# Two accumulating transfers per tile in place of GpSimd's additions, one state buffer per slot, and the last residuals kept on chip

## What is computed

```python
u = silu(conv(h) + b)                               # 512 inner channels
delta_lr, Bm = split(u @ x_proj_w.T + x_proj_b)     # Bm: 16 states
delta = softplus(delta_lr @ dt_w.T + dt_b)
deltaA = exp(einsum('bld,dn->bldn', delta, A))
deltaBu = einsum('bld,bln->bldn', delta * u, Bm)
def step(carry, inp):
    dA, dBu = inp
    carry = dA * carry + dBu
    return (carry, carry.sum(-1))                   # sum over the 16 states
y = ys + u * D_param
x = x + (y @ out_w.T + out_b)
```

## Time and profile before

| | us |
|---|---|
| median of 3 runs | 1076.79 |
| lowest and highest of them | 1074.73 and 1078.74 |
| the profiled execution, its own time | 1079.94 |
| its span, first to last instruction | 1078.2 |
| PE busy in the span | 959.9 (89%) |
| DVE busy | 897.8 (83%) |
| POOL busy | 859.3 (80%) |
| ACT busy | 755.8 (70%) |
| mean granted TensorE clock | 0.968 of full speed |

### The profile page before, as it was taken

The page is one execution under the profiler, slowest core; times in us unless marked ns, Lnnn a source line. Parts: engine busy times, 40 slices in busy tenths (PEclk is TensorE's granted clock), DMA queues, the critical chain, the costliest instruction groups (busy, mean ns, idle before and its releaser), DMA issues.

```text
span 1078.2 us, 13117 instructions
## 1 busy us (share of the span) xinstructions
PE 959.9 (89%) x4210; PEld 511.9 (47%) x4210; DVE 897.8 (83%) x1210; ACT 755.8 (70%) x1321; POOL 859.3 (80%) x617
## 2 busy tenths in 40 slices
PE   8786997999899999999889999899899999686976
PEld 6452453444545454545445454546355454432554
DVE  2433697899998999899989999799989999899944
ACT  2346558778698769877797769876887869765634
POOL 1357898988889888898889898889889888999700
PEclk9996999999999999999999999999999999899999
DMA  9813440434142430545042521344053202200000
GB/s 339 315 55 157 157 177 20 176 118 169 48 153 103 177 118 21 195 138 196 20 175 99 179 78 68 149 157 177 21 196 109 88 1 118 99 0 1 15 25 20
DMA packets 22059, 124.72 MB, mean 116 GB/s; under 512 B 3495, under 2 KB 4135, under 8 KB 9448
## 3 DMA queue, kind: packets, MB, share of 16 engines
q1 hardware_dynamic: 16376, 89.09, 22.7%
q10 hardware_dynamic: 5616, 34.81, 8.4%
HBM read 115.23 MB, written 8.65 MB: 115 GB/s over the span
## 4 chain that ended last, share of the span: by engine, by line
DVE 24%; POOL 21%; ACT 20%; PE 18%; issue 12%; DMA 4%; SPq 1%; ACTq 1%; DVEq 0%; POOLq 0%
POOL state L601 13%; DVE state L880 12%; PE bank L1013 10%; PE acc L1013 6%; ACT decay L668 5%; POOL state L609 4%; DVE raw L863 3%; DVE hm L943 2%; ACT u L759 2%; ACT soft L654 2%; DVE sg L930 2%; ACT L668 2%; ACT hid L654 2%; POOL x_in L570 2%; ACT u L767 1%
## 5 line engine op out<-in xcount | busy, mean ns | idle before, releaser
L601 POOL TENSOR_TENSOR state<-w,brep 128x512 f32<-128x512 f32 (+1 forms) x352 | 614.2, 1770 | 34.4 <-PE acc L1013 34.0
L880 DVE TENSOR_TENSOR_SCAN state<-decay,state 128x512 f32<-128x512 f32 (+1 forms) x352 | 590.7, 1696 | 44.6 <-ACT decay L668 26.1
L1013 PE MATMUL acc<-state,ident 128*128 128x512 f32 x832 | 406.8, 610 | 13.2 <-DVE state L880 9.3
L668 ACT ACTIVATE decay<-delta,neg_a 128x496 f32<-128x496 f32 x512 | 328.6, 671 | 97.8 <-DVE state L880 97.2
L1013 PEld LDWEIGHTS acc<-state,ident 128*128 128x128 f32 x832 | 150.4, 194 | 161.9 <-issue 118.8
L609 POOL TENSOR_TENSOR state<-state 128x512 f32<-128x512 f32 x96 | 122.3, 1274 | 29.5 <-DVE state L880 28.9
L695 ACT ACTIVATE sg<-bank,ag 128x512 f32<-128x512 f32 x64 | 43.5, 680 | 63.3 <-PE bank L1013 63.3
L1013 PE MATMUL bank<-xn_t,in_w 128*128 128x512 f32 x128 | 61.9, 619 | 13.1 <-ACT xn_t L716 7.8
L632 POOL TENSOR_TENSOR w<-delta,u 128x512 f32<-128x512 f32 x32 | 40.3, 1271 | 34.1 <-ACT delta L791 34.1
L1013 PE MATMUL bank<-out_w,u 128*128 128x256 f32 x256 | 58.0, 382 | 6.7 <-DVE u L871 6.7
L930 DVE SCALAR_TENSOR_TENSOR sg<-sg,bank 128x512 f32<-128x512 f32 x64 | 43.1, 674 | 18.2 <-ACT sg L695 18.2
(11 more groups left out here) (142 smaller groups left out, 1336.8 us busy)
## 6 DMA issues: line engine op xcount, KB each, us to landing
keys<-in_keys_t SPq DMA_DIRECT2D x32, 1028.0 KB, 4.8
keys<-in_keys_n SPq DMA_DIRECT2D x32, 1024.0 KB
brep<-b_scratch ACTq DMA_DIRECT2D x32, 1024.0 KB, 6.2
x_scratch<-x_in SPq DMA_DIRECT2D x8, 512.0 KB, 2.6
res<-x_scratch SPq DMA_DIRECT2D x8, 512.0 KB, 4.6
out<-res SPq DMA_DIRECT2D x8, 512.0 KB, 4.3
x_in<-in_x SPq DMA_DIRECT2D x7, 512.0 KB, 5.3
brep<-in_w_gateT SPq DMA_DIRECT2D x1, 1024.0 KB, 14.1
```

The costliest lines, as they stand in the source:

```text
L601: nc.gpsimd.tensor_tensor(state[state_buffer(odd, g)][:, 0:count, :], w[:, m, :].unsqueeze(1).to_broadcast((P, count, TOK)), brep[:, n:n + ...
L668: last = nc.scalar.activation(decay[:, to + i, :, 1:LEN], d, ACT.Exp, scale=neg_a[:, m, n + i:n + i + 1])
L880: nc.vector.tensor_tensor_scan(flat, decay[:, of:of + count, :, :].rearrange("p c q l -> p (c q l)"), flat, 0.0, ALU.mult, ALU.add).then_i ...
L1013: return nc.tensor.matmul(o, l, r, start=first, stop=last)
```

## The change

- `PAIRED` and POOL's additions are gone. `MERGED = {2: 0, 6: 4}`: when slot 2 is scanned, POOL issues a DMA transfer that reads both states of slot 0's buffer and adds them to the two states in slot 2's buffer; the same from slot 4 to slot 6. There are two of 512 KB per tile, 64 in the whole run, each waiting for the one before it. They are issued three slots behind POOL's inputs (`MERGE_LAG`).
- PE sums slots 2 and 6 four slots after their place (`MERGED_LAG`), with two matmuls each, and slots 0 and 4 not at all. That is 16 - 4 = 12 matmuls per tile. Those of slot 6 now stand together with slot 10's at the tile's end.
- State buffers: one per slot number, 11 of them, of one or two states.
- The residuals of the last two blocks are neither stored nor loaded; they stay in `x_in`, which `x2`, `stats3`, `xn3`, `finish` and the output store use in phases 8 and 9.
- `POST`, `PRE`, `LAST` and `PREPARE` have other steps for most parts.

```diff
 POST = [
-    ("x2", [4, 5]),  ("y_last", [0]),  ("finish", [32, 66, 76, 83]),
+    ("x2", [5, 5]),  ("y_last", [1]),  ("finish", [31, 65, 79, 84]),
 PRE = [
-    ("add1", [40]),  ("add2", [63]),  ("x_proj", [67]),  ("x_dbl", [72]),
-    ("dt", [73, 78, 85, 87]),  ("b_load", [77, 79, 79, 87]),
+    ("add1", [28]),  ("add2", [71]),  ("x_proj", [71]),  ("x_dbl", [73]),
+    ("dt", [75, 78, 87, 87]),  ("b_load", [77, 80, 87, 87]),
 PREPARE = [
-    ("quantise", [29, 48, 54, 57]),
+    ("quantise", [22, 57, 61, 72]),
...
-PAIRED = (2, 4, 6)
-PAIR_LAG = 4
-SUMS = [[k for k in range(CPT) if k + 2 * (k in PAIRED) == c] for c in range(CPT)]
+MERGED = {2: 0, 6: 4}
+MERGE_LAG, MERGED_LAG = 3, 4
+SUMS = [[k for k in range(CPT) if k not in MERGED.values() and k + MERGED_LAG * (k in MERGED) == c]
+        for c in range(CPT)]
...
-        state = [sb(f"state{i}", [P, 2, TOK]) for i in range(RING)]
+        state = [sb(f"state{c}", [P, SCAN[c][2], TOK]) for c in range(CPT)]
...
-                if post:
+                if post and pre:
                     reach(sp, out_stored, j - 2, 0)
                     sp.dma_start(res[:, :, :], t["x1_scratch"][j - 2]).then_inc(res_loaded, 16)
...
-                    reach(sp, res_biased[1], j, 1)
-                    sp.dma_start(t["x1_scratch"][j], x_in[par][:, :, :]).then_inc(x1_stored, 16)
+                    if j < BLOCKS - 2:
+                        reach(sp, res_biased[1], j, 1)
+                        sp.dma_start(t["x1_scratch"][j], x_in[par][:, :, :]).then_inc(x1_stored, 16)
...
-                        user = g - RING
-                        reach(pool, summed, *((b, sums_to(user)) if user >= 0 else (b - 1, sums_to(user + SLOTS))))
+                        user = g - CPT
+                        of, user = (b, user) if user >= 0 else (b - 1, user + SLOTS)
+                        if merge_from(user) is not None:
+                            reach(pool, merged, of, 16 * merges_to(merge_from(user)))
+                        else:
+                            reach(pool, summed, of, sums_to(user))
...
-                        done = g - PAIR_LAG
-                        if done >= 0 and done % CPT in PAIRED:
+                        done = g - MERGE_LAG
+                        if done >= 0 and done % CPT in MERGED:
+                            more = done - done % CPT + MERGED[done % CPT]
                             reach(pool, scan_done, b, done + 1)
-                            s = state[state_buffer(odd, done)]
-                            nc.gpsimd.tensor_tensor(s[:, 0, :], s[:, 0, :], s[:, 1, :], ALU.add).then_inc(paired, 1)
+                            if merges_to(done) > 1 or b:
+                                reach(pool, merged, b, 16 * (merges_to(done) - 1))
+                            nc.gpsimd.dma_start(state[done % CPT][:, :, :], state[more % CPT][:, :, :],
+                                                accum_op=ALU.add).then_inc(merged, 16)
...
-                            if k in PAIRED:
-                                reach(pe, paired, b, pairs_to(s))
+                            if k in MERGED:
+                                reach(pe, merged, b, 16 * merges_to(s))
                             else:
                                 reach(pe, scan_done, b, s + 1)
-                            for i in range(1 if k in PAIRED else SCAN[s][2]):
+                            for i in range(SCAN[s][2]):
```

More of the change, by code:

```diff
@@ L54 @@
-    ("out_proj", [2, 2]),
-    ("hidden", [15, 18, 21, 30, 43, 50, 64, 69]),
-    ("finish", [32, 66, 76, 83]),
-    ("x_evac", [13]),
-    ("scale_x", [12]),
-    ("down", [32, 57, 74, 80]),
+    ("x2", [5, 5]),
+    ("gate", [15, 17, 19, 23, 42, 50, 57, 69]),
+    ("xn3", [10]),
+    ("x_turn", [6]),
+    ("y_last", [1]),
+    ("rstd3", [4]),
+    ("stats3", [6]),
+    ("x_evac", [13]),
+    ("scale_h", [22, 33, 69, 79]),
+    ("out_proj", [2, 4]),
+    ("h_floor", [20, 31, 62, 76]),
+    ("h_scale", [22, 32, 69, 78]),
@@ L60 @@
+    ("h_evac", [30, 35, 75, 81]),
+    ("scale_x", [11]),
+    ("down", [32, 61, 78, 84]),
+    ("x_max", [10]),
+    ("h_turn", [26, 34, 72, 81]),
+    ("finish", [31, 65, 79, 84]),
+    ("tanh", [14, 18, 20, 22, 38, 49, 58, 68]),
+    ("h_max", [19, 29, 53, 71]),
+    ("up", [9, 14, 17, 22, 36, 46, 50, 67]),
+    ("hidden", [15, 18, 19, 26, 43, 51, 63, 69]),
 ]
 PRE = [
-    ("xn1", [5]),
-    ("query", [6]),
-    ("exp", [13, 19, 29, 37]),
-    ("softplus", [84, 87]),
-    ("x_dbl", [72]),
-    ("turn2", [55]),
@@ L86 @@
[L86 to L101 removed]
+    ("attn_out", [45, 47]),
@@ new lines @@
+    ("turn2", [54]),
+    ("evac2", [56]),
+    ("u_evac", [60, 61, 63, 65]),
+    ("xn2", [54]),
+    ("turn1", [4]),
+    ("p_evac", [18, 27, 31, 41]),
+    ("exp", [13, 22, 27, 38]),
+    ("softplus", [83, 87]),
+    ("p_sum", [19, 25, 31, 44]),
+    ("rstd1", [0]),
+    ("p_turn", [15, 25, 31, 40]),
+    ("zt_evac", [25, 29, 38, 44]),
+    ("add1", [28]),
+    ("p_last", [15, 24, 29, 38]),
+    ("tap0", [59, 61, 64, 65]),
+    ("add2", [71]),
+    ("attend", [23, 26, 32, 41]),
+    ("stats1", [2]),
@@ new lines @@
+    ("z_turn", [24, 27, 35, 44]),
+    ("mix_in", [57, 58, 59, 62]),
+    ("s_max", [13, 15, 25, 32]),
+    ("z_evac", [24, 27, 33, 43]),
+    ("xn1", [3]),
+    ("rstd2", [53]),
+    ("x_dbl", [73]),
+    ("times_u", [81, 87, 87, 87]),
+    ("s_neg", [13, 17, 25, 35]),
+    ("query", [5]),
+    ("stats2", [52]),
+    ("tap2", [59, 62, 65, 65]),
+    ("x1", [50, 51]),
+    ("evac1", [6]),
+    ("s_bias", [13, 19, 26, 38]),
+    ("x_proj", [71]),
+    ("dt", [75, 78, 87, 87]),
+    ("silu", [62, 65, 65, 65]),
@@ L121 @@
[L121 to L128 removed]
+    ("scale_x", [3]),
+    ("h_evac", [28, 41, 71, 80]),
+    ("h_floor", [26, 37, 57, 73]),
+    ("out_proj", [1, 11]),
+    ("hidden", [14, 24, 27, 36, 41, 53, 56, 72]),
+    ("h_scale", [29, 38, 72, 74]),
+    ("h_max", [25, 36, 56, 72]),
@@ L129 @@
+    ("x_evac", [5]),
+    ("x_turn", [11]),
+    ("down", [36, 39, 73, 74]),
+    ("x_max", [12]),
+    ("finish", [40, 44, 74, 74]),
+    ("x2", [1, 3]),
+    ("h_turn", [32, 38, 69, 69]),
+    ("stats3", [11]),
+    ("xn3", [1]),
+    ("y_last", [0]),
+    ("gate", [13, 14, 24, 28, 40, 44, 49, 70]),
+    ("tanh", [6, 14, 26, 26, 32, 41, 56, 56]),
+    ("rstd3", [11]),
+    ("scale_h", [26, 30, 58, 58]),
+    ("up", [21, 21, 26, 29, 36, 49, 50, 56]),
 ]
@@ L140 @@
 PREPARE = [
-    ("quantise", [29, 48, 54, 57]),
+    ("abs_sum", [5, 14, 14, 27]),
+    ("vo", [11]),
+    ("quantise", [22, 57, 61, 72]),
     ("vo_rep", [8]),
-    ("qk", [6]),
-    ("total", [35]),
-    ("scales", [42]),
-    ("vo", [7]),
-    ("vo_evac", [38]),
-    ("mixer_weights", [29]),
-    ("abs_sum", [8, 22, 24, 39]),
+    ("mixer_weights", [25]),
+    ("total", [27]),
+    ("scales", [36]),
+    ("vo_evac", [25]),
+    ("qk", [4]),
 ]
@@ L181, in sums_to, with merges_to, merge_from @@
     m, c = divmod(g, CPT)
-    return m * len(SUM_SLOTS) + SUM_SLOTS.index(c + 2 * (c in PAIRED)) + 1
-def pairs_to(g):
+    return m * len(SUM_SLOTS) + SUM_SLOTS.index(c + MERGED_LAG * (c in MERGED)) + 1
+def merges_to(g):
     m, c = divmod(g, CPT)
-    return m * len(PAIRED) + PAIRED.index(c) + 1
+    return m * len(MERGED) + list(MERGED).index(c) + 1
+def merge_from(g):
+    m, c = divmod(g, CPT)
+    return next((m * CPT + to for to, of in MERGED.items() if of == c), None)
 def slots_to(n):
```

105 lines of the change are left out of this document (20 added, 85 removed).

## The result

The changed kernel takes 1122.9 us (1122.2 to 1131.8) beside 1076.1 (1074.7 to 1078.7) for the one before: a ratio of 1.044, with a 95% interval of 1.041 to 1.047. It is 47 us slower; 12.5 us faster were forecast. The profiled execution took 1122.15, its span is 1120.3.

A forecast was written before the change was run, and what follows sets the result against it. No engine alone was taken as the bound: PE slightly latest, DVE right behind. Phases 2 to 7 gave 8.4 us less, phase 1 4, phase 8 1.5, tail 1.4 more: 12.5 less, median 1064; 8-in-10 range 1040 to 1096.

The forecast's parts named there:

- Other parts: Moved POST and PRE steps, quantise parts, residuals and tail; reordering priced 0, with 1 us a block either way.
- The period of a block: Steady block of 119.10 us: DVE becomes longest, block 2.4 us less before lateness; ends 0 and 5.2.
- The block: Steady block in phases 2 to 7: 2.4 less, minus 0.8 and 0.2 for transfers; marks about 117.7 us apart.
- POOL: Per block twelve additions (15.3 us) go, eight issues of 1.27 come: net 5.1 us less, 99.7 busy.
- Rival 2: An issue costs POOL more than the additions did, above 1.9 us; at 3.0 the total is 1093; chance 0.08.
- That wait costs nothing: POOL's wait for a scan at each merge is free while an issue stays under 5.7 us.
- The landing: An adding transfer lands in 4.6 to 6.2 us, 5.9 to 7.5 with its issue, hidden in most tiles.
- Rival 1: Transfers land too late, over 10.6 us after the scan, in six of ten of 32 tiles: 1096; chance 0.18.
- 0.8 + 0.2 a block: Late y at a block's last tile costs 0.8 us; shared DMA engines between output store and x2 0.2.
- Phase 1: First phase, where POOL leads: POOL's 5.1 us less are worth 4.
- The residuals: Dropped stores and loads of the last two residuals: worth 0.3 us, at the last x2.
- The tail: End of the last scan: y written 1.7 us later through slot 6's landing, net 1.4 more; ends -1 and 4.

The follow-up runs named there:

- a2: The kernel before with the changed kernel's four tables (POST, PRE, LAST, PREPARE), nothing else; 1126 us, ratio 1.048.
- d1: The kernel before with the whole new PRE table; 1141 us, ratio 1.059.
- b3: The kernel before with two PRE entries as in the changed one, attn_out [45, 47] and turn2 [54]; 1097.9 us, ratio 1.019.
- d4: b1 with slot 0's first state summed as well, 13 matmuls per tile in place of 12; 1098.5 us, ratio 1.020.
- b1: a4 with slots 2 and 6 summed in their own place, not four slots later; 1121.6 us, ratio 1.040.
- e1: The changed kernel with PE summing slot 0's first state, the transfer to slot 2 adding only the second; 13 matmuls per tile; 1132.5 us, ratio 1.053.
- d3: The kernel before without POOL's additions and its waits for them, three second states missing from the sum; 1074 us, ratio 0.998.
- b4: a3 with POOL's wait for the scans at the merges put back, still no transfers; 1109.6 us.
- a3: The changed kernel without its 64 transfers and POOL's scan waits for them, four of sixteen states missing from the sum; 1107.9 us, ratio 1.030.
- c3: The kernel before with only the residuals of its last two blocks kept in x_in; ratio 0.9999.
- d2: The kernel before with the new LAST and PREPARE tables alone; ratio 1.004.
- a4: a3 with the four tables of the kernel before; 1141 us, ratio 1.062.
- a1: The changed kernel with the four tables of the kernel before, transfers kept; 1173 us, ratio 1.091.
- c2: The kernel before with one spare matmul ahead of the first scores; 1076.2 us, ratio 1.0008.
- b2: The changed kernel with four spare matmuls in PE's gap ahead of turn2, in phases with a scan; 1112.2 us, ratio 1.030.
- c1: b2 with one more spare matmul, ahead of the first scores; 1113.3 us.
- e2: e1 with slot 4's first state summed directly too, both transfers 256 KB, 14 matmuls per tile; 1132.9 us, ratio 1.053.

## Why the prediction was wrong

**The step that failed** is the one under "Other parts": "The moved steps of POST and PRE are the same operations in another order; I take 0". By a2 the tables alone cost 52 us, by d1 `PRE` alone 64, and by b3 two of its entries 21. The trace before already had the place: the timeline of PE at `turn2` had 1.35 us of idle time behind ten records of sums, and the prediction didn't read it. Where "1 us a block either way" was allowed, a2 shows 6.9 (126.0 against 119.1).

**The step behind it** is "The period of a block": PE's 3.9 us less was taken as room for the others, with 0 as its worst end ("when other waits fill what PE frees"). That fewer sums could cost time was in no term and no rival. The sums are PE's filling between the stages of other work: one taken out of a place where PE waits for a chain of other engines frees nothing, and the clock can fall. The prediction read the clock as 0.99 and priced no fall of it. PE was to be busy 107.6 a block and was 111.0; its work did fall by the 3.9, and 3.5 of that came back as work at the lower clock. d4 against b1 is this step alone, in the old tables: one sum less per tile is 23 us slower. It isn't so in every order: e1 has one sum more than the changed kernel and is 10 us slower.

Point by point:
- The block: 117.7 forecast (1.4 less than 119.1), 124.2 measured. DVE, which was to become the longest, is busy 110 a block as before and idles 14.1 a block in place of 9.1.
- PE's records on `acc`: 768, as forecast. Price of 0.969 per matmul right at the upper level of the clock.
- POOL: the additions' 122.3 us went, 64 issues of 0.96 came where 1.27 was taken. A block is 7.9 us less in phases 2 to 7 ((629.6 - 582.0)/6) where 5.1 was said. Right in kind, and worth 2.7 us in all (d3). Rival 2, a dear issue, is out: no issue took over 1.18.
- "That wait costs nothing": right. POOL now waits 155.7 us for scans at the merges, and b4 shows that to be free.
- The landing, 4.6 to 6.2 forecast: 4.7 at the median, and 4.5 to 10.6 over the run. Rival 1 asked for over 10.6 us after the scan in six of ten tiles; it is one of the eight transfers of a block that lands so late. The forecast put the late one at the block's last tile behind the B loads. At the end of phase 1 it was right: landing in 9.54, 2.98 of waiting by PE, 4.49 by DVE. In phases 2 to 7 the late one was in the middle of the block, behind the keys and `x_in`; the last tile's landed in 6.0 to 6.7, and its y, now behind a scan, doesn't wait. The sum had 0.8 + 0.2 a block for them; the runs show 15 us in all (after against a3), of which 1.6 a block in phases 2 to 7 (124.2 against 122.6) and the rest in front of these.
- Phase 1, 4 less forecast. From its first scan to that of phase 2 it took 118.7 us (91.95 to 210.63) against 115.2 (93.35 to 208.56), 3.5 more. With the tables alone it took 115.1 (a2), without the transfers 115.9 (a3), so most of the 3.5 is theirs. POOL was the busiest there, as the prediction said, and its additions did go; but without them, and with nothing else changed, the phase took 114.2 (d3): a relief of 15.3 us of POOL's work brought 1.0, where 5.1 were to bring 4.
- The residuals: 0.3 forecast, none measured (c3, within 0.15%). `LAST` and `PREPARE`: 0 forecast, 3 us measured (d2).
- The tail: y waits 2.68 us for PE in place of 1.22, 1.5 more where 1.7 was forecast. That is luck: the forecast had it from the landing, but a3, without transfers, waits 2.68 as well, so it comes from slot 6's two matmuls, which now stand with slot 10's. From phase 8 to the end 0.5 more by `x2` and 4.2 by the first scan, against 0.1 less.

That wait at the end of the last scan:

```profile
1067.74 0.75 DVE L884 SCALAR_TENSOR_TENSOR u<-u,cols,acc 128x512 f32<-128x512 f32 x1 [2.68 <-PE acc L1030]
```

**The sum by the runs.** Beside the 1073.8 of before in the first comparison the changed kernel is 49 us slower: the tables in the old code give 52 (a2), the code with fewer sums and no additions or transfers takes 18 off again (a3 against a2), and the transfers put 15 on. In the old tables the same code without transfers costs 67 (a4) and the transfers 32 (a1). So the parts don't add up one by one: the new tables are bad for the old code and better than the old ones for the new code, by 50 us (a1 against after).

What stays open: which steps of `PRE`, besides the two of b3, make the 64 of d1; which steps make PE wait 2.3 us for a scan in each block of the changed kernel, a wait that is down to 0.2 in e1 without a gain; and why the clock falls behind the same gap in some versions and blocks and not in others. No version here beats the kernel before by more than 0.3%, and the one that does so (d3) leaves three states out of its sums.

## What to carry to other kernels

Where an engine's queue mixes the steps of one chain with filler from another, price each removed or moved filler at its place: read, in the timeline of that engine, what stands between a step and the next one that waits for other engines, and subtract. "The same operations in another order" is never 0 until the two or three places with idle time next to them have been compared. And where a gap grows past what the trace shows at full clock, add the slower matmuls behind it. Here the gap at `turn2` grew by 2.6 us a block, and the lower clock took 3.7 more, at this place and at the scores.

## What was not expected of the hardware

- After an idle stretch of PE of 3.9 us inside a busy kernel the granted clock was at 0.62, then 0.50 for two stretches of 2 us. Eight transposes took 1.97 us in place of 1.09, a sum 1.92 in place of 1.02. The clock fell at this place in every block with such a gap, and in every block of b1, whose gap was 2.19 (the transposes took 1.09 to 1.92). With 1.35 it fell in none of before, d3 and d4, and in five of six of c2; with 0.49 in none of b2 and c1. So the same work behind the same gap can run at either level.
- A transfer that adds one SBUF buffer to another, issued from GpSimd, kept POOL 876 to 1182 ns and landed in 4.5 us at the best, 4.7 at the median and 10.6 at the worst for 512 KB, counted from the start of its issue, and in 3.4 at the median for 256 KB (e2). By the Trainium skill (DMA: Bandwidth & Descriptors, Anatomy of one DMA, SWDGE path) an estimate of 3.2 had been worked out for 512 KB; all 64 were longer.
- Issues of such transfers stood on POOL while DVE scanned, with no longer issue than 1.18 us. By the Trainium skill (SBUF — State Buffer, SBUF: two separate sides) GpSimd can't write a transfer's descriptors while DVE is in a two-port mode. No such hold is seen in these rows.
